# Unpadded head projections spread by DMA, refilled rounds, and a line attention that starts during the loads

## The chip, the cores and the metric

The kernel runs on one core of a Trainium2 chip. The metric is the device time of one execution in microseconds (us).

## The reference

Two layers of a decoder on x, 16 batches of 112 tokens by 256 features, with a context of 16 x 375 x 128. Each layer is: an attention, a cross attention to the context, and a mixture of eight experts, each added to x after a layer norm.

```
x = x + line_attention(norm(x))                # layer 0: 16 heads, causal, Pluecker lines
x = x + cross(norm(x), ctx)                    # 16 heads of 16: softmax(q k^T / 4) v, then Wo
x = x + experts(norm(x))                       # top 2 of 8
x = x + linear_attention(norm(x))              # layer 1
x = x + cross(norm(x), ctx)
x = x + experts(norm(x))                       # top 1 of 8
# cross: q = x Wq + bq, k = ctx Wk + bk, v = ctx Wv + bv (layer 1 without the biases)
```

## The kernel before

Everything is float32. Stages follow one another, each a block with a program per engine and a barrier behind it: load_constants, line_attention (or linear_attention in layer 1), cross_attention, route, experts, combine.

**load_constants** (L178) starts x as one DMA and then nineteen of weights on SyncE's queue, and the context as four DMAs on ScalarE's. TensorE turns each batch's context in three transposes (L232), ScalarE and VectorE copy them into cT in turn (L222, L263). VectorE takes the statistics of all 16 batches of x (L257, L260). After a wait for all twenty (L265), TensorE makes two constant rows crow (bias of the values through the output weights, plus the output bias), one for each attention of layer 0, and VectorE scales the query weights by a quarter. Then the stage ends.

**line_attention** (L274) begins with the row scales on GpSimd (L153, L155), one row normed on VectorE (L160), and runs NB + 5 steps in which batch t is turned and projected (L335, L377), batch t - 1 gets its line coordinates on VectorE and their inverse norms by a power on GpSimd (L558), batch t - 2 its scores and exponentials, t - 3 its values and t - 4 its output product. GpSimd also adds the constant row to x (L555).

**cross_attention** (L562) is built from rounds. Head h lives on partition strip 32 * (h % 4): its 16 features lie on the first 16 partitions of the strip, and the weights are padded on the host with zero columns (head_columns, L1613), so that a projection of 128 columns gives four heads in place. A key projection of batch b is four products (keys, L680, `kT`), the queries eight (L668, `qT`). A round (round_of, L619) is the pair of score products of one batch (L610), whose maximum VectorE takes (L848), and the six transposed score products of the batch before it (L616), whose exponential ScalarE takes (L768). The maxima enter the transposed scores as a 17th row: the key side has ones there from its padded bias, the query side has the negated maxima, spread into a padded row tile (nmp, L862), turned by four transposes (L697, shift_turn) and added to the queries in `qs` (shifted_queries, L868). Scores have one pair of PSUM banks and so have the transposed scores: each round waits for the maximum and the exponential of the round before.

Eight rounds make the step of one batch. In step t, slots 0 to 4 take the score pairs 3 to 7 of batch t + 1 and slots 5 to 7 the pairs 0 to 2 of batch t + 2. Between the rounds TensorE has the rest, called filler here: values (L652), the turns of x (L661), keys, queries, context values (L690), the turn of the maxima, and of the output its turns and product (L705, L711, L717). The order is written out by hand:

```python
for t in range(-2, NB + 1):
    round_of(t, 0)   # behind it: values(t-1,3), x_turn(t+2)
    round_of(t, 1)   # keys(t+2,0), queries(t+2)
    round_of(t, 2)   # values(t,0), u_turn(t-1), keys(t+2,1)
    round_of(t, 3)   # keys(t+2,2)
    round_of(t, 4)   # values(t,1), out_turn(t-1), keys(t+2,3)
    round_of(t, 5)   # context_values(t+1,0) and (t+1,1)
    round_of(t, 6)   # values(t,2), out_product(t-1), context_values(t+1,2), shift_turn(t+1)
    round_of(t, 7)   # nothing
```

ScalarE copies keys (L784), context values (L791), turned x (L773), u and the output (L797, L802) between the exponentials, in layer 1 also the queries (L778); VectorE copies the queries in layer 0 (L856), normalises and adds the output to x. GpSimd adds the constant row. SyncE has nothing to do in this stage.

Of the kernel before, what the change touches and what calls it, by code (L numbers as in the profile page):

```python
# [177 lines left out]
def load_constants(nc, g, A):  # L178

    ph = Phase(nc, "load")  # L180
    s_x, s_w, s_pool, s_dve = ph.sem("x", "w", "pool", "dve")
    s_ctx = ph.sem("ctx0", "ctx1", "ctx2", "ctx3")
    turned, act_copied, dve_copied = ph.sem("turned", "act_copied", "dve_copied")
    made = ph.sem("made")
    bv = ph.sb("bv", [P, 4])
    bvb = ph.sb("bvb", [P, 4, S])
    spread = ph.sem("spread")
    st = ph.sb("st", [S, NB, 6])
    cin = ph.sb("cin", [CT, NB, NC3, CD])
    bt = [ph.ps(f"t{u}", [P, 512]) for u in range(4)]  # L190
    with nc.Block() as block:
        @block.sync
        def _(sp):
            sp.dma_start(g.x[:, :, :], A["x"].rearrange("b t d -> t b d")).then_inc(s_x, 16)
            sp.dma_start(g.w_l0[:, :, :], A["w_l0"].rearrange("(c p) n -> p c n", p=P)).then_inc(s_w, 16)
            sp.dma_start(g.wo_l0[:, :, :], A["wo_l0"].rearrange("(c p) n -> p c n", p=P)).then_inc(s_w, 16)
            for l in range(2):
                sp.dma_start(g.wq_x[:, l], A["wq_x"][l].rearrange("(c p) n -> p c n", p=P)).then_inc(s_w, 16)
                sp.dma_start(g.wo_x[:, l], A["wo_x"][l].rearrange("(c p) n -> p c n", p=P)).then_inc(s_w, 16)
                sp.dma_start(g.wr[:, l], A["wr"][l].rearrange("(c p) n -> p c n", p=P)).then_inc(s_w, 16)  # L200
            sp.dma_start(g.wk_x[:, :, :], A["wk_x"].rearrange("l p n -> p l n")).then_inc(s_w, 16)
            sp.dma_start(g.wv_x[:, :, :], A["wv_x"].rearrange("l p n -> p l n")).then_inc(s_w, 16)
            sp.dma_start(g.bq_x[:, :], A["bq_x"]).then_inc(s_w, 16)
            sp.dma_start(g.bk_x[:, :, :], A["bk_x"]).then_inc(s_w, 16)
            sp.dma_start(g.rows[:, :, :], A["rows"].rearrange("(o r) d -> o r d", o=1)).then_inc(s_w, 16)
            sp.dma_start(g.w_l1[:, :, :, :], A["w_l1"].rearrange("(c p) r n -> p c r n", p=P)).then_inc(s_w, 16)
            sp.dma_start(g.wo_l1[:, :, :], A["wo_l1"].rearrange("(c p) n -> p c n", p=P)).then_inc(s_w, 16)
            sp.dma_start(g.lepe[:, :, :], A["lepe"].rearrange("(m p) n -> p m n", p=P)).then_inc(s_w, 16)
            sp.dma_start(g.rope[:, :, :], A["rope"].rearrange("r t d -> t r d")).then_inc(s_w, 16)
            sp.dma_start(g.br[:, :, :], A["br"].rearrange("(o l) e -> o l e", o=1)).then_inc(s_w, 16)  # L210
            sp.dma_start(g.b2[:, :, :], A["b2"].rearrange("l e d -> e l d")).then_inc(s_w, 16)
            sp.dma_start(bv[:, :], A["bv"]).then_inc(s_w, 16)
            sp.wait_ge(s_w, 16 * 20)

        @block.scalar
        def _(act):
            for n in range(4):
                act.dma_start(cin[:, 4 * n:4 * n + 4].rearrange("p b c d -> p (b c) d"),
                              A["ctx"][4 * n:4 * n + 4].rearrange("b (c p) d -> p (b c) d", p=CT)).then_inc(s_ctx[n], 16)
            for b in range(0, NB, 2):  # L220
                act.wait_ge(turned, b + 1)
                act.activation(g.cT[:, b, :], bt[b % 4][:, 0:CL], ACT.Copy).then_inc(act_copied, 1)  # L222

        @block.tensor
        def _(pe):
            pe.wait_ge(s_pool, 3)
            for b in range(NB):
                if b % 4 == 0:
                    pe.wait_ge(s_ctx[b // 4], 16)
                reused(pe, (act_copied, dve_copied)[b % 2], (b - 4) // 2 + 1)  # L230
                for c in range(NC3):
                    last = pe.transpose(bt[b % 4][:, c * CT:(c + 1) * CT], cin[:, b, c, :], g.ident[0:CT, 0:CT])  # L232
                last.then_inc(turned, 1)
            pe.wait_ge(s_w, 16 * 20)
            pe.wait_ge(act_copied, NB // 2)
            pe.wait_ge(spread, 1)
            for r in range(2):
                for c in range(2):
                    pe.matmul(bt[0][0:S, r * D:(r + 1) * D], bvb[:, 2 * r + c, :],
                              g.wo_l0[:, c, :] if r == 0 else g.wo_x[:, 0, c, :], start=(c == 0), stop=False)  # L240
                pe.matmul(bt[0][0:S, r * D:(r + 1) * D], g.ones[0:1, 0:S], g.rows[0:1, r, :],
                          start=False, stop=True).then_inc(made, 1)

        @block.gpsimd
        def _(pool):
            pool.memset(g.ident[:, :], 0.0).then_inc(s_pool, 1)
            pool.memset(g.ones[:, :], 1.0).then_inc(s_pool, 1)
            pool.memset(g.nhalf[:, :], -0.5)
            pool.wait_ge(s_pool, 1)
            pool.affine_select(g.ident[:, :], g.ident[:, :], [[-1, P]], ALU.not_equal, 1.0, base=0,  # L250
                               channel_multiplier=1).then_inc(s_pool, 1)

        @block.vector
        def _(dve):
            dve.wait_ge(s_x, 16)
            for b in range(NB):
                dve.bn_stats(st[:, b, :], g.x[:, b, :]).then_inc(s_dve, 1)  # L257
            for b in range(NB):
                dve.wait_ge(s_dve, b + 1)
                dve.bn_aggr(g.mv[:, b, :], st[:, b, :])  # L260
            for b in range(1, NB, 2):
                dve.wait_ge(turned, b + 1)
                dve.tensor_copy(g.cT[:, b, :], bt[b % 4][:, 0:CL]).then_inc(dve_copied, 1)  # L263
            dve.wait_ge(s_w, 16 * 20)
            dve.tensor_copy(bvb[:, :, :], bv[:, :].unsqueeze(2).to_broadcast([P, 4, S])).then_inc(spread, 1)  # L265
            dve.wait_ge(made, 2)
            dve.tensor_copy(g.crow[:, :, :].rearrange("t r d -> t (r d)"), bt[0][0:S, 0:2 * D])
# [1396 lines left out]
```

## Time and profile before

| | us |
|---|---|
| median of 3 runs | 1896.82 |
| lowest, highest | 1896.57, 1900.24 |
| profiled execution | 1897.62 |
| its span | 1895.9 |

| engine | busy us | share of the span |
|---|---|---|
| TensorE, matmul | 1479.1 | 78% |
| TensorE, weight load | 1150.2 | 61% |
| VectorE | 802.7 | 42% |
| ScalarE | 584.7 | 31% |
| GpSimd | 348.0 | 18% |

Busy time is summed over stages with different limits. Matmuls are pipelined, so a busy TensorE isn't TensorE at its peak. A float32 product shows as two instructions. The granted clock is given as a share: 1.00 is 2.4 GHz and 0.50 is 1.2 GHz. In waits and timelines the part behind "<-" names what ended the idle time before an instruction.

### The profile page before, as it was taken

How to read it: one execution, taken by the hardware profiler on the slowest of the kernel's cores; microseconds unless marked ns; L12 is line 12 of the kernel's file. 1: busy time of each engine (PE TensorE's matmuls, PEld its weight loads, DVE VectorE, ACT ScalarE, POOL GpSimd, SP SyncE). 2: the span in 40 equal slices, each digit the busy share in tenths (PEclk: the TensorE clock that was granted, in tenths of full speed). 3: DMA queues.
4: the chain of work that ended last, by engine and by line, in shares of the span. 5: the costliest groups of instructions: out<-in, count | busy, mean ns of one | idle time of the engine just before them, and what ended most of it. 6: DMA issues, size and time to landing. Idle time of an engine off the chain costs nothing. (4 is left out here: it accounts for less than half of the span.)

```text
span 1895.9 us, 36053 instructions
## 1 busy us (share of the span) xinstructions
PE 1479.1 (78%) x14148; PEld 1150.2 (61%) x14148; DVE 802.7 (42%) x1935; ACT 584.7 (31%) x1278; POOL 348.0 (18%) x432
## 2 busy tenths in 40 slices
PE   0578779999997649999945666658999998649993
PEld 0355536667665539999923545536676676549991
DVE  1355534555552142222255666644545542132226
ACT  0166614554543112222201211114555554112220
POOL 0366510000000112323253111100000000112314
PEclk9699979999997569999957887759999998559995
DMA  7000000000000138898720000000000000138862
GB/s 184 20 1 2 2 1 2 2 2 2 2 2 1 39 152 330 319 333 320 291 65 17 0 0 0 1 1 1 2 2 2 2 2 2 39 146 323 327 250 80
DMA packets 39069, 154.82 MB, mean 82 GB/s; under 512 B 5311, under 2 KB 27167, under 8 KB 31776
## 3 DMA queue, kind: packets, MB, share of 16 engines
q0 software_dynamic: 13056, 130.53, 18.8%
q1 hardware_dynamic: 19868, 19.42, 3.5%
q10 hardware_dynamic: 6020, 3.07, 0.6%
q8 instruction: 95, 1.56, 0.3%
q14 instruction: 30, 0.25, 0.0%
HBM read 140.16 MB, written 12.85 MB: 81 GB/s over the span
## 5 line engine op out<-in xcount | busy, mean ns | idle before, releaser
L848 DVE TENSOR_REDUCE xa_mx<-xa_ps_s 112x2 f32<-112x750 f32 x256 | 240.3, 939 | 260.1 <-PE xa_ps_s L610 259.6
L616 PE MATMUL xa_ps_p<-xa_qs,xa_kT 32*125 32x112 f32 x3072 | 241.8, 289 | 59.7 <-DVE xa_mx L848 48.7
L616 PEld LDWEIGHTS xa_ps_p<-xa_qs,xa_kT 32*125 32x125 f32 x3072 | 198.6, 190 | 140.7 <-issue 69.5
L768 ACT ACTIVATE xa_p<-xa_ps_p 125x672 f32<-125x672 f32 x256 | 186.9, 730 | 226.5 <-PE xa_ps_p L616 226.5
L610 PE MATMUL xa_ps_s<-xa_kT,xa_qT 32*112 32x375 f32 x1024 | 232.2, 530 | 9.4 <-DVE xa_mx L848 9.2
L1439 PE MATMUL ex_ps_h<-ex_xT,ex_w 128*128 128x128 f32 x1792 | 212.8, 278 | 13.1 <-DMA ex_w<-in_experts,ex_now 13.0
L1439 PEld LDWEIGHTS ex_ps_h<-ex_xT,ex_w 128*128 128x128 f32 x1792 | 212.0, 195 | 17.0 <-DMA ex_w<-in_experts,ex_now 13.8
L1449 PE MATMUL ex_ps_y<-ex_w,ex_hT 128*128 128x256 f32 x896 | 202.7, 379 | 0.0
L1449 PEld LDWEIGHTS ex_ps_y<-ex_w,ex_hT 128*128 128x128 f32 x896 | 166.0, 190 | 20.1
L1472 ACT ACTIVATE ex_hT<-ex_ps_h,ex_w 128x128 f32<-128x128 f32 x224 | 69.9, 363 | 290.4 <-PE ex_ps_h L1439 290.4
L1484 DVE TENSOR_SCALAR ex_hT<-ex_ps_h,ex_w 128x128 f32<-128x128 f32 x224 | 68.2, 346 | 175.1 <-PE ex_ps_h L1439 150.3
L680 PE MATMUL xa_ps_a<-cT,wk_x 128*128 128x375 f32 x256 | 113.4, 527 | 0.1
L652 PE MATMUL xa_ps_o<-xa_p,xa_v 125*17 125x112 f32 x3072 | 102.4, 268 | 1.7 <-ACT xa_p L768 1.7
L153 POOL TENSOR_SCALAR rstd<-mv 112x16 f32<-112x16 f32 x6 | 1.7, 286 | 548.1 <-POOLq L77 452.4
L558 POOL TENSOR_TENSOR line_inv<-line_ss,nhalf 112x32 f32<-112x32 f32 x16 | 87.1, 5444 | 53.6 <-DVE line_ss L487 53.6
L1492 DVE COPY ex_y<-ex_ps_y 128x256 f32<-128x256 f32 x56 | 23.7, 424 | 167.6 <-PE ex_ps_y L1449 167.6
L784 ACT ACTIVATE xa_kT<-xa_ps_a,bk_x 128x375 f32<-128x375 f32 x128 | 73.4, 573 | 62.5 <-PE xa_ps_a L680 61.9
L610 PEld LDWEIGHTS xa_ps_s<-xa_kT,xa_qT 32*112 32x112 f32 x1024 | 71.4, 172 | 20.4 <-issue 10.4
L1553 PE MATMUL cb_ps_b<-b,wtT 8*112 8x256 f32 x64 | 36.5, 675 | 53.8 <-DVE cb_sum L1561 43.8
L652 PEld LDWEIGHTS xa_ps_o<-xa_p,xa_v 125*17 125x17 f32 x3072 | 68.3, 99 | 16.6 <-ACT xa_p L768 2.1
L668 PEld LDWEIGHTS xa_ps_a<-xa_xT,wq_x 128*128 128x128 f32 x512 | 69.9, 212 | 10.0 <-issue 2.9
L1398 POOL COPY ex_now<-xrow 128x1 int32 (+1 forms) x58 | 10.6, 183 | 347.9 <-PE ex_ps_y L1449 228.8
(258 smaller groups left out, 2164.3 us busy)
## 6 DMA issues: line engine op xcount, KB each, us to landing
ys<-ex_y SPq DMA_DIRECT2D x56, 128.0 KB
xn<-rt_xn SPq DMA_DIRECT2D x8, 448.0 KB, 4.4
load_cin<-in_ctx ACTq DMA_DIRECT2D x4, 750.0 KB
x<-in_x SPq DMA_DIRECT2D x1, 1792.0 KB
out_x<-x SPq DMA_DIRECT2D x16, 112.0 KB
wq_x<-in_wq_x SPq DMA_DIRECT2D x2, 512.0 KB
w_l<-in_w_l SPq DMA_DIRECT2D x1, 1024.0 KB
ex_xg<-xn,ex_now POOLq DMA_INDIRECT x56
```

The lines of the kernel that those rows point to most:

```text
L558: pool.tensor_tensor(inv[:, b % 2], ss[:, b % 2], g.nhalf[:, :], ALU.pow).then_inc(inv_done, 1)
L610: return pe.matmul(bsc[0:S, i, 0:CL], qT[r:r + 32, b % 2, n, :], kT[r:r + 32, b % KB, n, :], start=True, stop=True)
L616: return pe.matmul(bp[0:CT, i, c * S:(c + 1) * S], kT[r:r + 32, b % KB, n, c * CT:(c + 1) * CT], qs[r:r + 32, b % 2, n, :], start=True, st ...
L652: last = pe.matmul(bo[32 * j:32 * j + HD + 1, n * S:(n + 1) * S], vb[:, b % VB, c, h, :], p[slot % 4][:, j % 2, c * S:(c + 1) * S], start= ...
L668: last = pe.matmul(ba[0][:, n * S:(n + 1) * S], g.wq_x[:, layer, c, n * P:(n + 1) * P], xT[:, c, :], start=(c == 0), stop=(c == 1))
L680: pe.matmul(ba[(1, 1, 0, 1)[n]][:, 0:CL], g.wk_x[:, layer, n * P:(n + 1) * P], g.cT[:, b, :], start=True, stop=True).then_inc(k_made, 1)
L768: act.activation(p[slot % 4][:, :, :], bp[0:CT, :, 0:NC3 * S], ACT.Exp).then_inc(exped, 1)
L784: act.activation(kT[:, b % KB, n, :], ba[(1, 1, 0, 1)[n]][:, 0:CL], ACT.Identity, bias=g.bk_x[:, layer, n:n + 1]).then_inc(k_copied, 1)
L848: dve.tensor_reduce(mx[:, b % 2, 2 * pair:2 * pair + 2], bsc[0:S, :, 0:CL], AX, ALU.max).then_inc(maxed, 1)
L1439: last = pe.matmul(bh[k][:, (j % 2) * SLOTS:(j % 2 + 1) * SLOTS], w[:, u, c * FF + j * P:c * FF + (j + 1) * P], xT[:, c, :], start=(c == 0 ...
L1449: last = pe.matmul(by[u % 2][:, 0:D], hT[:, u % 2, j, :], w[:, u, 2 * FF + FJ + j * D:2 * FF + FJ + (j + 1) * D], start=(j == 0), stop=(j ...
L1472: last = act.activation(hT[:, u % 2, 2 * k + i, :], bh[k][:, i * SLOTS:(i + 1) * SLOTS], ACT.Relu, bias=bias(u, 2 * k + i))
```

## The change

Load stage. It is gone as a stage. All loads are issued by SyncE inside the block of the line attention, in the order x (four DMAs of four batches, each with its own semaphore), the line weights, `bv` and `rows` (line_in), then the cross weights and the context (cross_in), then the rest. The context is turned on the host and loaded into cT directly. VectorE takes the statistics of four batches before the steps and of four more in each of steps 0, 1 and 2; GpSimd makes the row scales in four groups. The first constant row is made in step 0 of the line attention, behind the first projection, the second at the start of the first cross attention. The query weights are no longer scaled; the factor is in the copy of the queries.

Cross attention. Weights are unpadded. Keys are two products of 128 columns (eight heads each) copied to `kU`, queries four products copied by VectorE to `qU`. SyncE spreads them from there to the strips of `kT` and `qT` (three buffers each): eight DMAs per key half, eight for the queries, and four that put the negated maxima, turned by a single narrow transpose and copied by ScalarE to `nmT`, onto row 16 of each strip. The ones on the key side are from a memset of `kT`. `qs` and its addition are gone. Score products contract 16 rows and transposed ones 17. TensorE waits for the DMAs at rounds 0, 1 and 5. The filler is arranged anew and the loop begins one step earlier.

```diff
+def load_constants(sp, g, A):
+    for n in range(4):
+        rows = slice(4 * n, 4 * n + 4)
+        sp.dma_start(g.x[:, rows, :], A["x"][rows].rearrange("b t d -> t b d")).then_inc(g.x_in[n], 16)
+    sp.dma_start(g.w_l0[:, :, :], A["w_l0"].rearrange("(c p) n -> p c n", p=P)).then_inc(g.line_in, 16)
+    sp.dma_start(g.wo_l0[:, :, :], A["wo_l0"].rearrange("(c p) n -> p c n", p=P)).then_inc(g.line_in, 16)
...
+    for n in range(4):
+        sp.dma_start(g.cT[:, 4 * n:4 * n + 4, :], A["ctxT"][:, 4 * n:4 * n + 4, :]).then_inc(g.cross_in, 16)
...
# line attention, VectorE
+            row_stats(0)
...
             for t in range(NB + 5):
+                if t < 3:
+                    row_stats(t + 1)
+                if t == 1:
+                    dve.wait_ge(crow_made, 1)
+                    dve.tensor_copy(g.crow[:, 0, :], b_out[0:S, 0:D]).then_inc(crow_set, 1)
...
# cross attention, SyncE
+            def spread_k(b, m):
+                sp.wait_ge(k_copied, 2 * b + m + 1)
+                reused(sp, shifted, PAIRS * (b - RB + 1))
+                sp.wait_ge(ones_set, b % RB + 1)
+                for k in range(2):
+                    for j in range(4):
+                        i = 4 * k + j
+                        sp.dma_start(kT[32 * j:32 * j + HD, b % RB, 2 * m + k, :], kU[HD * i:HD * i + HD, b % 2, m, :]) \
+                            .then_inc(k_spread[RB * m + b % RB], 16)
...
+            def spread_nm(b):
+                sp.wait_ge(nm_copied, b + 1)
+                reused(sp, shifted, PAIRS * (b - RB + 1))
+                for j in range(4):
+                    sp.dma_start(qT[32 * j + HD:32 * j + HD + 1, b % RB, :, :], nmT[QUADS * j:QUADS * j + QUADS, b % 2, :]) \
+                        .then_inc(nm_spread[b % RB], 16)
+            for t in range(-2, NB):
+                if on(t + 2):
+                    spread_k(t + 2, 0)
+                    spread_q(t + 2)
+                if on(t + 1):
+                    spread_nm(t + 1)
+                if on(t + 2):
+                    spread_k(t + 2, 1)
# cross attention, TensorE
-                return pe.matmul(bsc[0:S, i, 0:CL], qT[r:r + 32, b % 2, n, :], kT[r:r + 32, b % KB, n, :],
+                return pe.matmul(bsc[0:S, i, 0:CL], qT[r:r + HD, b % RB, n, :], kT[r:r + HD, b % RB, n, :],
...
-                    if slot == 0:
-                        pe.wait_ge(qs_made, t + 1)
+                    if slot == 0:
+                        pe.wait_ge(nm_spread[t % RB], 16 * NM_DMAS * (t // RB + 1))
...
+                        pe.wait_ge(q_spread[sb % RB], 16 * Q_DMAS * (sb // RB + 1))
+                    if sp % 4 == 0:
+                        pe.wait_ge(k_spread[RB * (sp // 4) + sb % RB], 16 * K_DMAS * (sb // RB + 1))
```

The new order of the filler:

```python
for t in range(-3, NB + 1):
    round_of(t, 0)   # behind it: values(t-1,3), keys(t+2,0)
    round_of(t, 1)   # queries(t+2)
    round_of(t, 2)   # values(t,0), u_turn(t-1)
    round_of(t, 3)   # context_values(t+1,0) and (t+1,1)
    round_of(t, 4)   # values(t,1), context_values(t+1,2)
    round_of(t, 5)   # keys(t+2,1), shift_turn(t+1)
    round_of(t, 6)   # values(t,2), out_turn(t-1)
    round_of(t, 7)   # x_turn(t+3), out_product(t-1)
```

## Rows read from the trace of the kernel before

**Rows 1.** Timeline, load stage and first projection: start, us, engine, line, operation, count.

```profile
0.82 45.34 ACTq L218 DMA_DIRECT2D load_cin<-in_ctx  x4
...
0.82 0.39 SPq L194 DMA_DIRECT2D x<-in_x  x1
...
17.57 5.32 DVE L257 BATCH_NORM_STATS2 load_st<-x 112x6 f32<-112x256 f32 x16 [17.57 <-DMA x<-in_x]
...
60.22 0.38 DVE L265 COPY load_bvb<-load_bv 128x448 f32<-128x448 f32 x1
...
76.13 3.67 PE L377 MATMUL line_ps_b<-w_l,line_xT 128*112 128x512 f32 x4 [0.45 <-ACT line_xT L417]
```

**Rows 2.** Windows, load stage: busy of PE, PEld, DVE, ACT, POOL; clock, DMA, GB/s.

```profile
10.00:17.60 7.60, 0.00 (x0) 0.00 (x0) 0.03 (x1) 0.00 (x0) 0.00 (x0) 1.00 1.11 261
```

**Rows 3.** Timeline, ScalarE, copies of u: one per batch, first and second cross stage.

```profile
428.40 0.54 ACT L797 ACTIVATE xa_uT<-xa_ps_o 128x448 f32<-128x448 f32 x1
...
448.65 0.54 ACT L797 ACTIVATE xa_uT<-xa_ps_o 128x448 f32<-128x448 f32 x1
...
1495.59 0.54 ACT L797 ACTIVATE xa_uT<-xa_ps_o 128x448 f32<-128x448 f32 x1
...
1515.83 0.54 ACT L797 ACTIVATE xa_uT<-xa_ps_o 128x448 f32<-128x448 f32 x1
```

**Rows 4.** Timeline of one cross batch: a round with nothing behind it, and the next.

```profile
446.97 0.36 PE L616 MATMUL xa_ps_p<-xa_qs,xa_kT 32*125 32x112 f32 x2 [1.12 <-DVE xa_mx L848]
...
447.92 0.94 DVE L848 TENSOR_REDUCE xa_mx<-xa_ps_s 112x2 f32<-112x750 f32 x1 [1.09 <-PE xa_ps_s L610]
...
449.01 0.36 PE L616 MATMUL xa_ps_p<-xa_qs,xa_kT 32*125 32x112 f32 x2
```

**Rows 5.** Timeline, same batch: TensorE, queries, one filled round, the output product.

```profile
430.33 1.93 PE L668 MATMUL xa_ps_a<-xa_xT,wq_x 128*128 128x112 f32 x16
...
432.20 0.36 PE L616 MATMUL xa_ps_p<-xa_qs,xa_kT 32*125 32x112 f32 x2
...
433.04 0.77 PE L652 MATMUL xa_ps_o<-xa_p,xa_v 125*17 125x112 f32 x24
...
434.22 0.80 PE L680 MATMUL xa_ps_a<-cT,wk_x 128*128 128x375 f32 x2
...
434.95 0.36 PE L616 MATMUL xa_ps_p<-xa_qs,xa_kT 32*125 32x112 f32 x2
...
443.07 1.12 PE L717 MATMUL xa_ps_m<-wo_x,xa_aoT 128*112 128x256 f32 x4
```

**Rows 6.** Timeline and one line's view: what a DMA issue costs on SyncE.

```profile
21.77 0.53 SPq L204 DMA_DIRECT2D bk_x<-in_bk_x  x1
...
27.08 0.99 SPq L210 DMA_DIRECT2D br<-in_br  x1
...
L1513 SPq DMA_DIRECT2D ys<-ex_y x56: 332/332/377, 707.1 to 1848.3; - x56
```

**Rows 7.** Waits of SyncE: us in total, times, longest; the last store of the program.

```profile
SPq L1531 <- DMA out_x<-x: 1.4, 1, 1.4
```

**Rows 8.** Windows of the first cross stage: steady state, lead-in, tail (columns as in 2).

```profile
430.00:450.00 20.00, 18.43 (x271) 13.91 (x270) 10.65 (x18) 9.99 (x18) 0.72 (x1) 1.00 0.01 2
...
275.00:279.00 4.00, 3.49 (x14) 1.21 (x13) 2.44 (x5) 1.15 (x2) 0.72 (x1) 1.00 0.00 0
...
588.00:592.00 4.00, 3.18 (x43) 2.37 (x42) 0.00 (x0) 1.46 (x2) 0.00 (x0) 0.52 0.02 4
```

**Rows 9.** Timeline, start of the first cross stage and its first shifted scores.

```profile
246.80 0.26 POOL L153 TENSOR_SCALAR rstd<-mv 112x16 f32<-112x16 f32 x1 [19.98 <-SPq L604]
...
283.76 0.36 PE L616 MATMUL xa_ps_p<-xa_qs,xa_kT 32*125 32x112 f32 x2 [1.12 <-DVE xa_mx L848]
```

**Rows 10.** Timeline, tail of that stage: twelve shifted scores at the lower clock.

```profile
595.40 1.60 PE L616 MATMUL xa_ps_p<-xa_qs,xa_kT 32*125 32x112 f32 x12 [0.83 <-ACT xa_p L768]
```

**Rows 11.** Timeline: the power that makes the row scales, sixteen columns.

```profile
70.16 2.95 POOL L155 TENSOR_TENSOR rstd<-rstd,nhalf 112x16 f32<-112x16 f32 x1
```

More of the change, by code:

```diff
@@ L147, in persistent @@
     g.yrow = sb("yrow", [S, 2, NB], I32)
+    g.loads = Phase(nc, "loads")
+    g.x_in = g.loads.sem("x0", "x1", "x2", "x3")
+    g.line_in, g.cross_in, g.rest_in = g.loads.sem("line", "cross", "rest")
     return g
@@ L175, in add_to_x @@
     dve.tensor_copy(g.mv[:, bass.ds(b, 1), :], mv).then_inc(s_x, 1)
[L178 to L267, printed above, removed]
-            dve.tensor_scalar(g.wq_x[:, :, :, :].rearrange("p l c n -> p (l c n)"),
-                              g.wq_x[:, :, :, :].rearrange("p l c n -> p (l c n)"), CROSS_SCALE, None, ALU.mult)
-            dve.tensor_scalar(g.bq_x[:, :], g.bq_x[:, :], CROSS_SCALE, None, ALU.mult)
-    ph.close()
@@ L318, in line_attention, with _ @@
     with nc.Block() as block:
+        @block.sync
+        def _(sp):
+            load_constants(sp, g, A)
         @block.tensor
@@ L385, in u_turn, with constant_row @@
                 last.then_inc(u_turned, 1)
-            pe.wait_ge(set_v, 5)
-            pe.wait_ge(set_p, 2)
+            def constant_row():
+                pe.wait_ge(spread, 1)
+                for c in range(2):
+                    pe.matmul(b_out[0:S, 0:D], g.bvb[:, c, :], g.wo_l0[:, c, :], start=(c == 0), stop=False)
+                pe.matmul(b_out[0:S, 0:D], g.ones[0:1, 0:S], g.rows[0:1, 0, :], start=False, stop=True).then_inc(crow_made, 1)
+            pe.wait_ge(ident_set, 3)
             for t in range(NB + 5):
@@ L718, in out_product @@
                 last.then_inc(out_made, 1)
-            pe.wait_ge(set_v, 2)
-            pe.wait_ge(set_p, 1)
-            for t in range(-2, NB + 1):
+            pe.wait_ge(set_v, 2 - layer)
+            pe.wait_ge(v_set, 1)
+            if layer == 0:
+                pe.wait_ge(g.cross_in, 16 * CROSS_DMAS)
+                for c in range(2):
+                    pe.matmul(bm[0:S, 0:D], g.bvb[:, 2 + c, :], g.wo_x[:, 0, c, :], start=(c == 0), stop=False)
+                pe.matmul(bm[0:S, 0:D], g.ones[0:1, 0:S], g.rows[0:1, 1, :], start=False, stop=True).then_inc(crow_made, 1)
+            for t in range(-3, NB + 1):
                 round_of(t, 0)
@@ L804, in _ @@
             act.activation(warm[:, :], g.mv[:, 0, 0:1], ACT.Exp)
-            for t in range(-2, NB + 1):
+            for t in range(-3, NB + 1):
                 if on(t):
```

353 lines of the change are left out of this document (209 added, 144 removed).

## The prediction

> **What bounds the kernel now.** The profiled execution took 1897.62 us with a span of 1895.9, so 1.7 us lie around the span; the median of the runs shown is 1896.82, 0.8 us under it. The sum is made against 1897.6 and then carried to the median unchanged. I read the time by stage, because the change touches only some: the load stage, both cross attentions, and the entry of the line attention. Router, experts, combine and linear attention keep their code.
>
> The load stage is a wait. x is read as one transfer and lands at 17.6 us, the last of the twenty weights lets VectorE go on at 60.2, the context occupies ScalarE's queue for 45 us, and the first projection of the line attention starts at 76.1 [rows 1]. TensorE has nothing to win here; what counts is which bytes the first projection really needs.
>
> The cross attentions take one batch each 20.25 us in both layers [rows 3] at the full clock, with TensorE busy 18.4 of 20 us against 10.7 and 10.0 for VectorE and ScalarE [rows 8]. A batch is eight rounds. A round with nothing behind it takes 2.04 us: 446.97 to 449.01, the loop from the scores over VectorE's 0.94 us maximum back to the same PSUM banks [rows 4]. A round with filler takes 0.84 us (432.20 to 433.04) plus the filler: the next starts at 434.95, 2.75 us on, after values, four turns and one key product [rows 5]. So up to 1.2 us of filler per round is free and the rest is paid. Before, filler is bunched: eight bare rounds are 16.3 us, and the 3.9 us to 20.25 are filler above the free amount in four rounds, while one is empty.
>
> **The change, part by part.**
>
> *Less filler, spread.* Four padded key products become two, at 0.73 us each (434.22 to 434.95), sixteen query passes become eight, 1.87 us (430.33 to 432.20) to some 0.93, and four turns of the maxima become one narrow one [rows 5]. By slot the filler is then: slot 0 values and keys, 0.77 + 0.73 = 1.50; slot 1 queries, 0.93; slot 2 values and four turns, 1.18 (433.04 to 434.22); slot 7 the output product and two turns, about 1.2 by its 1.12 [rows 5]; slots 3 to 6 a pair of small products each, under 1.2 by the same prices. Only slot 0 exceeds the free amount: 0.84 + 1.50 = 2.34, and seven at 2.04 give 16.6 us. What hides the filler is VectorE's loop; it must keep its own extra work (queries 0.4 us, normalise, finish) inside the gaps of a round, which 10.7 busy us in 16.6 allow.
>
> *28 DMAs per batch on SyncE.* Eight for each key half, eight for the queries, four for the row of maxima. Their operands must land before a round, where before a VectorE or ScalarE copy in place sufficed. Price of an issue: 0.33 us where the queue is free, 0.53 and 0.99 for two small ones of the load stage, the latter onto a single partition [rows 6]. I take 0.36 with the step between two (0.04) for the 24 wide ones, which look like the first, and 0.57 for the four that write one partition; the bounds are 0.36 and 1.0. From the end of an issue to its landing: the last store is waited for 1.4 us [rows 7]; a small copy inside SBUF can hardly need more, and I let it go to 2. The queue order is keys 0, queries, maxima, keys 1, and SyncE waits in that order, so a late maxima row delays keys 1 behind it. Two paths: (a) round 0 to keys 0 copied, about 3.1 us (an estimate: the burst, values and product of rows 5, then ScalarE's copy); 16 issues 5.8; landing 1.4: 10.3, due for round 5, which starts at 2.34 + 4 x 2.04 = 10.5. Just hidden. (b) From round 5 to the maxima copied 2.65 us (an estimate: burst and key product of rows 5, then ScalarE's exponential and two short copies), four issues 2.3, eight issues 2.9, landing 1.4: 9.2 us; it is due for round 1 of the next step, 3 x 2.04 + 2.34 = 8.5 after round 5. So 0.7 us shows, and a batch takes 17.3. With all issues at 0.36 it is 8.4, hidden: 16.6. With 1.0 for the four it is 10.9: 19.0.
>
> Thirteen batches per layer run in this state: 13 x (20.25 - 17.3) = 38 us, 77 for both layers.
>
> *The prologue.* From the start of the stage to the first shifted scores are 37.0 us now [rows 9]. The new one has the DMAs in series with nothing to cover them: 16 issues and a landing, 7.2 us, before the first score, and the maxima row, 3.7 us, before the first shifted score; the shorter projections and the overlap of the second batch's give part back. Bounds 2 and 8, I take 6 per layer, 12. In the first layer the constant row (three products and a copy) moved here from the load stage: 3 us. The gain of the cross stages is 77 - 12 - 3 = 62.
>
> The Trainium skill, "DMA: Bandwidth & Descriptors", section "Rules for kernel authors", speaks against this part: small transfers are to be coalesced, since under 64 KB one pays mostly overhead, and "Anatomy of one DMA" puts a fixed 2 us on each. The last store's 1.4 us [rows 7] is below it. By the page's 2 us path (b) ends 0.6 us later and the batch is an estimated 17.9 us.
>
> *Load stage.* The first projection needs x and the line weights. In order on one queue are now x, 512 KB and 256 KB and two small ones, 2.56 MB in all, ahead of everything else; at the 261 GB/s of the stretch before x landed [rows 2] 9.8 us, plus 0.8 at the start and 1.4 landing: 12. At two thirds of that rate it is 17. I take 14 for the first projection instead of 76.1 [rows 1]: 62 us. Row statistics and scales of the first four batches lie before it: four statistics at a sixteenth of 5.3 us each, and a power of four columns under the 2.95 of sixteen [rows 11], all done about 10 us. Given back: the other twelve statistics on VectorE, 3 x 2 us, three powers of about 1.2 on GpSimd, which already carries that loop, and the constant row of 3 us on TensorE before the second turn. I take 8 (bounds 3 and 14). The later weights and the context (now 128 partitions, no transposes, no copies) have 170 us to land. Gain 62 - 8 = 54, bounds 45 and 62. The memsets of the key tiles are on GpSimd beside the row scales' wait; cover gone, they would cost some 1.5 us once.
>
> **Sum:** 1897.6 - 62 - 54 = 1781.6; I give 1781.
>
> **The rivals.**
>
> *The SyncE queue sets the batch.* Issues at 0.47 instead of 0.36 and at 1.0 for the four, landing 2: path (b) is 2.65 + 4 + 3.8 + 2 = 12.5, the batch 8.16 + 12.5 = 20.6, so the cross stages lose 9 + 15, and only the load gain is left: 1868. Half of that surcharge, a batch of 19, gives 1897.6 - (32 - 15) - 54 = 1826. For it: four rows of the load stage over 0.9 would fit; against: fifty-six stores at 0.332 with 128 rows each [rows 6].
>
> *TensorE falls to the lower clock in the steady state* (the slower side). What holds the clock is not shown by busy time alone: it stood at 1.00 in the lead-in with 3.49 of 4 us busy and fell to 0.52 in the tail with 3.18 of 4, where only shifted scores and values ran [rows 8]. Now contractions are 16 and 17 rows high instead of 32 and full-array projections are halved. At the lower clock twelve shifted scores take 1.60 us [rows 10] while the whole burst with its scores lasts 0.84 now [rows 5], so a burst is some 1.6 and the 9 us of filler per batch about 16: 12.8 + 16 = 29 us, 26 x 8.7 = 226 us more, 1897.6 + 226 + 15 - 54 = 2085. It is slower than before from a mean batch of 21.8 us on, that is when four batches in ten run at the lower clock ((21.8 - 17.3) / (29 - 17.3)). Against: rounds are fuller, 15.5 busy of 17.3.
>
> The Trainium skill, "TensorE: Matmul & The Clock Gate", section "HAM oscillation — how this bites in real kernels", has the same effect for idle gaps between bursts; the lead-in and tail [rows 8] agree that the level moves with what TensorE did before.
>
> *The early start does not deliver.* If the 17.6 us of x [rows 1] is the queue's pace and not shared with the context, the projection starts at 26: 12 us less, 1793; with 14 given back 1799.
>
> *Strips of 16 or 17 rows do not run side by side.* Then the change does not do what it says and the bursts double: about 1.7 us a round, 8 x 0.85 more where not hidden, batch 23 or so, 1897.6 + 72 + 15 - 54 = 1930. Against: values of 17 columns share the array, 24 in 0.77 us [rows 5].
>
> **How the numbers follow.** Forecast (batch 16.6 to 18, load 45 to 62): 1750 to 1810, 0.62. SyncE sets the batch: 0.20, 1815 to 1868. Early start short: 0.08. Lower clock: 0.06. Strips: 0.04. 1781 is the first. The range 1745 to 1832 takes the first, the third and half of the second and leaves out 0.2. Faster 0.89, within 0.2% (what a measurement of this kernel can tell from no change) 0.01, slower 0.10, the last two rivals.
>
> **What would show it.** ScalarE's copies of u 16.6 to 17.5 us apart; keys' and maxima's DMA waits on TensorE under 1 us per batch; SyncE's issues near 0.33; the first projection near 14 us and the line attention's later batches as far apart as before; the clock 1.00 in the steady state. Wrong would be copies 19 us or more apart, with TensorE waiting for DMA at rounds 0, 1 and 5, or a clock near 0.5 in the middle of a cross stage.

## The result, and the profile after

The changed kernel takes 2138.9 us (median of four, 2135.8 to 2142.6) against 1897.1 us (the median of the kernel before, with one run more than in its table): 1.128 times as long, 95% interval 1.126 to 1.129. The forecast was 1781. The profiled execution has a span of 2140.4 us, 244.5 more than the 1895.9 before.

The page of the changed kernel, its first lines and the products of the cross attention (busy us, mean ns of one, idle before):

```profile
span 2140.4 us, 35951 instructions
PE 1787.9 (84%) x13620; PEld 1335.5 (62%) x13620; DVE 782.3 (37%) x1909; ACT 547.4 (26%) x1222; POOL 357.6 (17%) x444
PEclk8995555555555559999858887555555555558995
L648 PE MATMUL xa_ps_s<-xa_kT,xa_qT 16*112 16x375 f32 x1024 | 403.0, 884 | 28.0 <-DMA xa_qT<-xa_qU 20.8
L654 PE MATMUL xa_ps_p<-xa_qT,xa_kT 17*125 17x112 f32 x3072 | 405.3, 429 | 22.0 <-DMA xa_qT<-xa_qU 7.9
```

TensorE does less work than before and is busy for longer: the clock row stands at 5 tenths over both cross stages. Before, the steady state was at 1.00 [rows 8]. Windows of the changed kernel in the first cross stage (us, busy of PE, PEld, DVE, ACT, POOL, then the granted clock):

```profile
300.00:360.00 60.00, 60.00 (x519) 42.53 (x522) 20.05 (x32) 18.85 (x34) 1.45 (x2) 0.50 0.08 19
360.00:420.00 60.00, 60.00 (x524) 42.67 (x518) 20.05 (x32) 18.85 (x34) 1.45 (x2) 0.50 0.08 19
454.00:458.00 4.00, 3.94 (x69) 3.22 (x68) 2.80 (x6) 1.33 (x2) 0.00 (x0) 1.00 0.15 36
458.00:462.00 4.00, 3.19 (x46) 2.06 (x46) 1.99 (x3) 2.46 (x5) 0.00 (x0) 1.00 0.12 27
462.00:466.00 4.00, 0.81 (x12) 0.84 (x14) 0.00 (x0) 0.00 (x0) 0.00 (x0) 0.68 0.09 18
466.00:470.00 4.00, 4.00 (x31) 2.50 (x25) 0.94 (x1) 1.44 (x3) 0.00 (x0) 0.50 0.00 0
```

60.00 of 60 us busy at 0.50 is the lower of the clock's two levels (1.2 GHz), with no gap to blame. Twice it rose for some 10 us, once in each cross stage. The first time is at 454 to 462: there the rounds follow each other as planned, and then a transfer comes late. The timeline of that stretch:

```profile
454.88 0.57 PE L648 MATMUL xa_ps_s<-xa_kT,xa_qT 16*112 16x375 f32 x2
457.00 0.57 PE L648 MATMUL xa_ps_s<-xa_kT,xa_qT 16*112 16x375 f32 x2
459.03 0.57 PE L648 MATMUL xa_ps_s<-xa_kT,xa_qT 16*112 16x375 f32 x2
458.25 5.64 SPq L624 DMA_DIRECT2D xa_qT<-xa_qU  x8
465.19 0.55 PE L654 MATMUL xa_ps_p<-xa_qT,xa_kT 17*125 17x112 f32 x2 [3.94 <-DMA xa_qT<-xa_qU]
```

A batch is read from ScalarE's copies of u (a batch's products with its values, before they are divided by the sums), as in [rows 3]; the first three and the last of the first layer:

```profile
272.67 0.54 ACT L834 ACTIVATE xa_uT<-xa_ps_o 128x448 f32<-128x448 f32 x1 [0.45 <-PE xa_ps_o L689]
303.15 0.54 ACT L834 ACTIVATE xa_uT<-xa_ps_o 128x448 f32<-128x448 f32 x1 [0.45 <-PE xa_ps_o L689]
332.74 0.54 ACT L834 ACTIVATE xa_uT<-xa_ps_o 128x448 f32<-128x448 f32 x1 [0.45 <-PE xa_ps_o L689]
703.99 0.54 ACT L834 ACTIVATE xa_uT<-xa_ps_o 128x448 f32<-128x448 f32 x1 [2.52 <-PE xa_ps_o L689]
```

The first step is 30.5 us, and from then on nearly every step of both layers is 29.6, where 20.25 stood before. The load part, by contrast, did what was asked. The timeline of the changed kernel: first projection, start of the cross stage, the constant row, the first scores and the first shifted scores.

```profile
12.63 3.72 PE L324 MATMUL line_ps_b<-w_l,line_xT 128*112 128x512 f32 x4 [2.64 <-DMA rows<-in_rows]
188.52 0.20 ACT L841 ACTIVATE xa_warm<-mv 112x1 f32<-112x1 f32 x1 [4.22 <-PEq L76]
192.17 2.02 PE L757 MATMUL xa_ps_m<-wo_x,bvb 128*112 128x256 f32 x4 [5.76 <-POOL xa_v L947]
210.28 1.59 PE L648 MATMUL xa_ps_s<-xa_kT,xa_qT 16*112 16x375 f32 x4 [10.44 <-DMA xa_qT<-xa_qU]
242.76 0.55 PE L654 MATMUL xa_ps_p<-xa_qT,xa_kT 17*125 17x112 f32 x2 [0.57 <-DVE xa_mx L879]
```

So the 244.5 us divide as follows (us; "u" is a batch's copy of u, and the last column is the last kernel of the experiments):

| interval | before | changed | last experiment |
|---|---|---|---|
| to the first cross stage | 246.8 | 188.5 | 188.4 |
| stage start to first u, layer 0 | 60.1 | 84.2 | 71.4 |
| first to last u, layer 0 | 302.9 | 431.3 | 264.4 |
| last u to first u of layer 1 | 703.6 | 725.5 | 712.6 |
| first to last u, layer 1 | 301.5 | 430.4 | 260.0 |
| last u to the end | 281.0 | 280.5 | 281.7 |
| span | 1895.9 | 2140.4 | 1778.4 |

58.3 us are gained in the load part, 46.0 lost on the way into the two stages (24.1 and 21.9), 257.3 lost from copy to copy. On the way in, the first scores wait 10.44 us for the query copies, as the row above shows, and the whole stretch runs at 0.50.

### The profile page after: what moved, and what is told of

Read it like the earlier page. It is cut to its first block and busy times, and to the rows that moved or that the text cites. A ratio compares the mean times of both kernels' runs of the same rounds, so it can differ in the third digit from the quotient of the medians.

```text
span 2140.4 us, 35951 instructions
## 1 busy us (share of the span) xinstructions
PE 1787.9 (84%) x13620; PEld 1335.5 (62%) x13620; DVE 782.3 (37%) x1909; ACT 547.4 (26%) x1222; POOL 357.6 (17%) x444
## 5 line engine op out<-in xcount | busy, mean ns | idle before, releaser
L654 PEld LDWEIGHTS xa_ps_p<-xa_qT,xa_kT 17*125 17x125 f32 x3072 | 338.4, 315 | 162.3 <-issue 123.9
L648 PE MATMUL xa_ps_s<-xa_kT,xa_qT 16*112 16x375 f32 x1024 | 403.0, 884 | 28.0 <-DMA xa_qT<-xa_qU 20.8
L654 PE MATMUL xa_ps_p<-xa_qT,xa_kT 17*125 17x112 f32 x3072 | 405.3, 429 | 22.0 <-DMA xa_qT<-xa_qU 7.9
L1486 PEld LDWEIGHTS ex_ps_y<-ex_w,ex_hT 128*128 128x128 f32 x896 | 165.9, 190 | 20.2
L689 PE MATMUL xa_ps_o<-xa_p,xa_v 125*17 125x112 f32 x3072 | 167.0, 384 | 0.0
L648 PEld LDWEIGHTS xa_ps_s<-xa_kT,xa_qT 16*112 16x112 f32 x1024 | 114.3, 278 | 45.0 <-DMA xa_qT<-xa_qU 22.8
L689 PEld LDWEIGHTS xa_ps_o<-xa_p,xa_v 125*17 125x17 f32 x3072 | 106.5, 137 | 33.4 <-issue 25.9
L706 PE MATMUL xa_ps_k<-cT,wk_x 128*128 128x375 f32 x128 | 103.3, 911 | 0.0
L954 POOL TENSOR_TENSOR x<-x,crow 112x256 f32<-112x256 f32 x16 | 11.6, 724 | 412.7 <-DVE xa_xn L164 412.7
L725 PE MATMUL xa_ps_x<-wv_x,cT 128*125 128x256 f32 x128 | 75.7, 693 | 0.0
L1004 PE MATMUL lin_ps_b<-ident,lin_xn 112*128 112x112 f32 x32 | 9.2, 388 | 72.0 <-DVE lin_xn L164 72.0
## 6 DMA issues: line engine op xcount, KB each, us to landing
xa_kT<-xa_kU SPq DMA_DIRECT2D x512, 23.4 KB, 1.9
```

The costliest lines, as they stand in the source:

```text
L648: return pe.matmul(bsc[0:S, i, 0:CL], qT[r:r + HD, b % RB, n, :], kT[r:r + HD, b % RB, n, :], start=True, stop=True)
L654: return pe.matmul(bp[0:CT, i, c * S:(c + 1) * S], kT[r:r + HD + 1, b % RB, n, c * CT:(c + 1) * CT], qT[r:r + HD + 1, b % RB, n, :], start ...
L689: last = pe.matmul(bo[32 * j:32 * j + HD + 1, n * S:(n + 1) * S], vb[:, b % VB, c, 4 * n + j, :], p[slot % 4][:, j % 2, c * S:(c + 1) * S] ...
L706: pe.matmul(bk[:, 0:CL], g.wk_x[:, layer, m * P:(m + 1) * P], g.cT[:, b, :], start=True, stop=True).then_inc(k_made, 1)
L725: pe.matmul(bank[0:CT, 0:D], g.cT[:, b, c * CT:(c + 1) * CT], g.wv_x[:, layer, :], start=True, stop=True).then_inc(v_made, 1)
L1486: last = pe.matmul(by[u % 2][:, 0:D], hT[:, u % 2, j, :], w[:, u, 2 * FF + FJ + j * D:2 * FF + FJ + (j + 1) * D], start=(j == 0), stop=(j ...
```

## The experiments

Theory H (the height of the contraction): products over 16 and 17 rows, with half of the full-array products gone, do not keep the clock up, however busy TensorE is. Rival F: the halved filler alone does it. Rival Q: the waits for SyncE's copies and the long empty start let the clock fall. A cost beside them, whatever the clock, is the SyncE queue itself. A batch below is the usual distance of two copies of u, and the clock is read in stretches of 20 us. "Filler" says how much full-height key and query work a batch has against the kernel before: "doubled" is the changed kernel's half, issued twice. e1, e2 and e6 to e9 have one run each, e3, e4, e5 and e10 four; the kernel before, run beside them, had medians of 1897.9 to 1900.1 us, and ratios below are to these, with their 95% intervals.

| kernel | rows | filler | copies | clock in the steady state | batch, us | time, us |
|---|---|---|---|---|---|---|
| before | 32 | full | none | 1.00 | 20.25 | 1897 |
| e1 | 16/17 | full | none | 1.00, later 0.74 to 0.93 | 20.2, later 23 | 1994 |
| changed | 16/17 | half | 28, SyncE | 0.50, two short rises | 29.6 | 2139 |
| e2 | 32 | half | 28, SyncE | 0.81 to 0.99 | 23.7 | 1969 |
| e9 | 16/17 | doubled | 28, SyncE | 0.50 to 1.00 | 24 to 36 | 2149 |
| e3 | 32 | half | 28, two queues | 1.00, at times 0.83 | 19.1 | 1834 |
| e4 | 32 | full | none | 1.00 | 20.2 | 1843 |
| e5 | 32 | half | 20, two queues | 1.00 | 18.1 | 1800 |
| e6 | 16/17 | half | as e5 | 0.50, two short rises | 29.6 | 2106 |
| e7 | 16/32 | half | as e5 | 1.00, at times 0.5 | 18, at times 28.7 | 1850 |
| e8 | 16/17 | doubled | as e5 | 1.00, once 0.91 | 18.9, at times to 21.5 | 1889 |
| e10 | 32 | half | 20, three queues | 1.00 | 17.3 | 1780 |

**e1: the height alone, in the kernel before.**

```diff
-  pe.matmul(bsc[0:S, i, 0:CL], qT[r:r + 32, ...], kT[r:r + 32, ...],
+  pe.matmul(bsc[0:S, i, 0:CL], qT[r:r + HD, ...], kT[r:r + HD, ...],
...
-  pe.matmul(bp[0:CT, i, ...], kT[r:r + 32, ...], qs[r:r + 32, ...], ...)
+  pe.matmul(bp[0:CT, i, ...], kT[r:r + HD + 1, ...], qs[r:r + HD + 1, ...], ...)
```

> The kernel before, in which only the height of the contraction in the two small products is changed: scores 16 rows instead of 32, shifted scores 17 instead of 32. The rows left out hold zeros, so instruction counts, columns and results stay. Theory H (the height): products of 16 and 17 rows, side by side, do not hold the clock. It expects the granted clock near 0.5 in both cross stages, the copies of u some 33 to 35 us apart (18.4 busy us of the batch nearly double) instead of 20.25, and 2250 to 2300 us. Rival F (filler: the halved full-array projections) and rival Q (waits for the new DMAs let the clock fall) expect the clock at 1.00 and 1897 us, since this kernel has neither.

1993.8 us, 96 more for leaving out rows that hold zeros. Windows of its first cross stage:

```profile
345.00:365.00 20.00, 18.43 (x272) 13.80 (x270) 10.66 (x17) 10.20 (x18) 0.72 (x1) 1.00 0.01 2
385.00:405.00 20.00, 18.52 (x227) 13.73 (x229) 9.28 (x15) 9.23 (x17) 0.72 (x1) 0.83 0.00 1
525.00:545.00 20.00, 19.31 (x209) 14.56 (x212) 7.55 (x12) 8.18 (x15) 0.72 (x1) 0.74 0.00 1
```

Up to 385 us it is the same kernel as before, busy time and all, at 1.00; then the clock goes up and down, and most batches take 22 to 25 us. Rivals F and Q, which both said 1897, are out as the whole cause; so is H in its strong form, which said 0.5 throughout and 2250 to 2300. The height has an effect, and full filler resists it.

**e2: the changed kernel with 32 rows.** The queries' slot is zeroed by GpSimd once a batch.

```diff
+  pool.memset(qT[:, b % RB], 0.0).then_inc(q_zeroed, 1)
...
-  qT[r:r + HD, b % RB, n, :], kT[r:r + HD, b % RB, n, :],
+  qT[r:r + 32, b % RB, n, :], kT[r:r + 32, b % RB, n, :],
```

> The changed kernel with both small products contracted over 32 rows again: the slot of the queries is zeroed by one GpSimd memset a batch, the key pads hold ones, so the rows added contribute zero. DMAs, filler and order stay. Theory H expects the clock at 1.00 for most of both cross stages and a batch set by SyncE's chain at its measured issue cost of 0.63 us, 20 to 22 us: 26 x (29.6 - 21) = 224 us less than 2139, near 1915. Rival F expects the clock to stay at 0.50 and 2139. Rival Q expects 0.50 as long as TensorE waits 4 us for a DMA in some batches, so also near 2139, or a mixture.

1968.7 us: 170 of the 241.8 us of the loss come back with two heights changed in the products, though GpSimd does more. Rival F, which said 2139, is out here too. Its windows, and the waits of TensorE in 300 to 420 (us in total, times, longest):

```profile
300.00:360.00 60.00, 47.85 (x688) 35.19 (x684) 25.95 (x41) 24.10 (x45) 2.32 (x4) 0.91 0.09 21
360.00:420.00 60.00, 45.48 (x634) 33.84 (x626) 25.16 (x40) 22.57 (x41) 3.48 (x6) 0.89 0.11 25
```

```profile
PE xa_ps_p L655 <- issue: 18.3, 5, 4.2
PE xa_ps_p L655 <- DMA xa_qT<-xa_qU: 6.6, 5, 1.5
```

Busy share is lower than in the changed kernel (46.7 of 60 against 60.00) and the clock higher. The rows put 18.3 us to "issue", idle time for which the profile shows no releaser. These waits stand before the rounds that need the second key half, fall to 6.0 us in the same stretch of e3, where SyncE issues sixteen copies a batch, and are gone in e5, where it issues twelve; that they are waits for the second key half is inferred from this. A batch is 23.7 us, not the 20 to 22 expected; how much of the excess is the queue and how much the clock of 0.9 was not separated.

**e3: two queues.** e2 with the twelve copies of queries and maxima issued by GpSimd.

```diff
-  sp.dma_start(qT[32 * j:32 * j + HD, b % RB, k:QUADS:2, :], qU[HD * i:HD * i + HD, b % 2, :, :])
+  pool.dma_start(qT[32 * j:32 * j + HD, b % RB, k:QUADS:2, :], qU[HD * i:HD * i + HD, b % 2, :, :])
...
-  sp.dma_start(qT[32 * j + HD:32 * j + HD + 1, b % RB, :, :], nmT[QUADS * j:QUADS * j + QUADS, b % 2, :])
+  pool.dma_start(qT[32 * j + HD:32 * j + HD + 1, b % RB, :, :], nmT[QUADS * j:QUADS * j + QUADS, b % 2, :])
```

> As the run before it (32-row contractions), and the eight query copies and four maxima copies of each batch are issued from GpSimd's queue, so that SyncE issues only the 16 key copies, at 0.63 us each 10.1 us a batch. Theory H with the SyncE chain as the second cost: clock 1.00 and a batch of 16.6 to 18 us, so 1897 - 26 x 2.8 + 15 - 58 = 1780, range 1760 to 1820. If issues on GpSimd cost as much as on SyncE and the maxima's path stays late, 19 us a batch and 1830. Rival F expects 0.50 and about 2100.

1834.3 us (ratio 0.966, interval 0.964 to 0.968), 19.1 us a batch: above the 1760 to 1820 of the theory and at the 1830 given for late maxima. A window of it:

```profile
300.00:360.00 60.00, 50.36 (x767) 36.27 (x765) 31.07 (x52) 28.48 (x53) 21.84 (x42) 1.00 0.12 28
```

GpSimd's issues are cheaper than SyncE's (504 ns for the queries, 524 for the maxima, against 589), and a batch still waits for the queries (1.0 to 1.4 us), for the second key half by the inference above (1.2 to 1.4) and in part of the batches for the maxima (up to 1.7).

**e4: the new load part with the old cross attention.** In the changed kernel the whole cross attention is the old one again, the scaling aside, which is now done as the queries are copied.

```diff
-  kU = ph.sb("kU", [P, 2, 2, CL])
-  qU = ph.sb("qU", [P, 2, 2, S])
...
+  qs = ph.sb("qs", [P, 2, QUADS, S])
```

> The load stage and the line attention of the changed kernel with the cross attention of the kernel before (padded projections, 32-row contractions, no copies between partitions; the scaling of the query weights is moved into the copy of the queries, and the constant rows are made where the changed kernel makes them). It measures the load part alone: the first cross stage began 58.3 us earlier in the changed kernel, so 1897 - 58 = 1839, 1835 to 1845 with the constant row in the first cross stage. If the load gain is given back in a later stage, it shows as a time nearer 1897. A clock of 1.00 and 20.25 us a batch in both cross stages is expected by every theory.

1843.1 us (0.971, 0.970 to 0.973), inside the range expected. Two of its copies of u:

```profile
353.26 0.54 ACT L799 ACTIVATE xa_uT<-xa_ps_o 128x448 f32<-128x448 f32 x1
373.51 0.54 ACT L799 ACTIVATE xa_uT<-xa_ps_o 128x448 f32<-128x448 f32 x1
```

The stage starts at 187.8, batches are 20.2 us apart at 1.00, and the two parts of the change are now separate: the load part is worth 55 us, the cross part costs 296 (2138.9 less 1843.1).

**e5: fewer copies.** One copy carries both key halves, so that eight do the work of sixteen; for that the second half's product moves one step earlier, and the maxima are back on SyncE. 32 rows.

```diff
-  sp.dma_start(kT[32 * j:32 * j + HD, b % RB, 2 * m + k, :], kU[HD * i:HD * i + HD, b % 2, m, :])
+  sp.dma_start(kT[32 * j:32 * j + HD, b % RB, k:QUADS:2, :], kU[HD * i:HD * i + HD, b % 2, :, :])
```

> The 32-row kernel with fewer and better spread copies: both key halves of a batch are projected before their copies, so that one copy carries both (8 instead of 16 a batch, on SyncE), the four maxima copies are on SyncE and the eight query copies stay on GpSimd. In the run before it the three waits of a batch were 1.4 us (queries), 0.2 to 1.7 us (maxima) and 1.3 us (second key half). Theory (32 rows hold the clock; what is left above the bare rounds is late copies): clock 1.00 in the steady state, 16.6 to 17.5 us a batch instead of 19.1, so 1834 - 26 x 2.1 = 1780, range 1765 to 1800. If a copy with twice the rows costs twice the issue (1.2 us), nothing is gained: 19 to 20 us and 1835 to 1850.

1800.5 us (0.947, 0.943 to 0.950), 18.1 us a batch, 0.6 above the range. A copy that carries both halves costs the same issue (595 ns against 589), so eight issues a batch are saved; what the merger alone is worth, without the other two moves, was not run. The Trainium skill, "DMA: Bandwidth & Descriptors", section "Rules for kernel authors", asks for small transfers to be coalesced; this trace agrees, by issues saved. One wait is left, the queries'; TensorE's waits in 280 to 400:

```profile
PE xa_ps_p L643 <- DMA xa_qT<-xa_qU: 8.7, 7, 1.6
```

**e6: e5 with 16 and 17 rows.**

```diff
-  qT[r:r + 32, b % RB, n, :], kT[r:r + 32, b % RB, n, :],
+  qT[r:r + HD, b % RB, n, :], kT[r:r + HD, b % RB, n, :],
...
-  kT[r:r + 32, b % RB, n, c * CT:(c + 1) * CT], qT[r:r + 32, b % RB, n, :],
+  kT[r:r + HD + 1, b % RB, n, c * CT:(c + 1) * CT], qT[r:r + HD + 1, b % RB, n, :],
```

> The kernel of the run before it in this set with one difference: the contractions are 16 rows (scores) and 17 rows (shifted scores) instead of 32; the rows left out hold zeros on the query side. Copies, queues, waits and filler are the same. Theory H (height, with the halved full-array filler): the clock stays at 0.50 through both cross stages, 29 to 30 us a batch, 2120 to 2140 us. Rival Q (waits for copies and the long empty prologue let the clock fall in the changed kernel): with most of those waits gone the clock is at 1.00 and the time that of the 32-row kernel within 5 us.

2105.8 us against 1800.5 for one difference. Its windows:

```profile
300.00:360.00 60.00, 58.60 (x547) 42.09 (x550) 20.73 (x33) 19.91 (x37) 10.98 (x22) 0.54 0.10 20
360.00:420.00 60.00, 60.00 (x523) 42.39 (x516) 20.52 (x34) 19.03 (x35) 10.33 (x20) 0.50 0.09 18
```

The clock had risen for one batch (22.6 us long) and fell again, around one wait of 1.3 us, where e5 keeps 1.00 through seven waits of up to 1.6 us; then 29.6 us a batch to the end of the layer. In layer 1 it rose once more, and there a batch took 17.6 us, near the forecast's 17.3:

```profile
1640.00:1660.00 20.00, 18.88 (x272) 13.76 (x267) 10.31 (x17) 9.38 (x18) 4.62 (x10) 0.92 0.13 27
```

So this kernel can run at either level; what made the clock rise there is open. As the main cause rival Q is refuted: taking most of the waits away recovers 33 of the 242 us and leaves the clock at 0.50 nearly throughout.

**e7: the scores alone at 16 rows**, on e5.

```diff
-  qT[r:r + 32, b % RB, n, :], kT[r:r + 32, b % RB, n, :],
+  qT[r:r + HD, b % RB, n, :], kT[r:r + HD, b % RB, n, :],
```

> As the 32-row kernel with merged copies, but the scores alone contract 16 rows; the shifted scores keep 32. It tells whether a part of the height is enough. A score has 375 columns and a pair of them is 750 column passes a round, four shifted-score strips side by side 672: if the clock follows the mean height of all passes, this lies halfway: clock alternating, 20 to 24 us a batch, 1870 to 1970 us. If either product alone holds the clock, 16.6 to 17.5 us a batch and the 32-row time; if both are needed, 0.50 and 2120 to 2140.

1850.4 us, where 1870 to 1970 was expected. Its windows, a good and a bad stretch:

```profile
360.00:420.00 60.00, 55.20 (x827) 40.21 (x826) 31.98 (x52) 29.79 (x56) 15.52 (x30) 0.96 0.14 27
420.00:480.00 60.00, 59.17 (x688) 42.40 (x687) 27.83 (x45) 24.90 (x45) 15.51 (x30) 0.73 0.14 27
```

Between the two cases, but much nearer the 32-row kernel (1800.5) than e6 (2105.8), and mostly at 1.00. So the clock does not simply follow the mean height of all products, as the expectation had it. The shifted scores alone at 17 rows were not run.

**e8: e6 with the filler of the kernel before.** Every key and query product is issued twice into the same place.

```diff
+  for again in range(2):
+      last = pe.matmul(bk[:, 0:CL], g.wk_x[:, layer, m * P:(m + 1) * P], g.cT[:, b, :], ...)
...
-  for m in range(2):
+  for m in (0, 1, 0, 1):
```

> As the kernel with 16 and 17 rows and merged copies, but every key product and every group of query products is issued twice with the same operands into the same place, so that the full-height filler per batch is again that of the kernel before (four key products, sixteen query passes); results do not change. Theory H with the filler as its second part: the clock rises for part of the time as in the kernel before with 16 and 17 rows (0.83 to 1.00 by stretches, 22 to 25 us a batch), so 1930 to 2030 us although more work is done. If only the height of the small products matters, 0.50 and more work: 31 to 33 us a batch and 2180 to 2220 us.

1888.5 us: 192 more products than e6 (384 instructions), none of them needed, and 217 us less. Windows and two copies of u:

```profile
300.00:360.00 60.00, 58.80 (x846) 43.10 (x850) 31.06 (x50) 29.36 (x55) 15.46 (x30) 1.00 0.14 27
420.00:480.00 60.00, 58.23 (x833) 42.72 (x829) 31.73 (x51) 29.11 (x55) 16.61 (x32) 1.00 0.14 28
```

```profile
346.19 0.54 ACT L823 ACTIVATE xa_uT<-xa_ps_o 128x448 f32<-128x448 f32 x1
365.11 0.54 ACT L823 ACTIVATE xa_uT<-xa_ps_o 128x448 f32<-128x448 f32 x1
```

Steadier and faster than expected (22 to 25 us a batch). Height and filler thus act together: with these copies, low products with half the filler stay near 0.50, and either one restored brings the clock back. It also bears on e1, which has the same heights and as many full-height projections but alternates. There the filler is bunched and rounds stand bare; that this is the reason is likely, and was not tried by itself.

**e9: the changed kernel with doubled filler.**

```diff
+  for again in range(2):
+      last = pe.matmul(bk[:, 0:CL], g.wk_x[:, layer, m * P:(m + 1) * P], g.cT[:, b, :], ...)
...
+  for m in (0, 1, 0, 1):
```

> The changed kernel itself with one difference: every key product and every group of query products is issued twice with the same operands into the same place, so the full-height filler per batch is again four key products and sixteen query passes. Heights of 16 and 17 rows, all 28 copies on SyncE and their waits stay. If the missing filler alone keeps it at the lower clock, the clock rises and the batch is set by SyncE's chain: 22 to 24 us and 1940 to 1990, faster than 2139 although more work is done. If the waits for SyncE's copies are needed as well for the fall, it alternates as the changed kernel with 32 rows did (clock 0.81 to 0.93, 23.7 us a batch): 1970 to 2050. If the height alone keeps it down, 0.50 and 31 to 33 us a batch: 2180 to 2220.

2148.7 us, in none of the three ranges: the clock alternates, as the second said, but lower and with batches of 24 to 36 us, 100 us above its time; from the changed kernel's 2139 one run does not tell it apart. Windows:

```profile
360.00:420.00 60.00, 54.01 (x537) 38.34 (x536) 20.14 (x33) 18.60 (x34) 1.45 (x2) 0.70 0.08 19
540.00:600.00 60.00, 50.55 (x660) 36.69 (x660) 24.56 (x40) 23.19 (x44) 2.18 (x3) 0.92 0.09 22
```

Doubled filler holds 1.00 in e8 and not here, and what differs is the copies, their queues and the waits for them (up to 3.7 us for the queries between 300 and 600 us, 1.3 in e8). So rival Q has a share after all: it cannot explain the 0.50, but where the products are low the late copies undo what the filler brings. Which of the differences does it was not tried.

**e10: three queues.** e5 with two of the eight query copies issued by ScalarE and six by GpSimd, and a wait moved out of the stage's start; 32 rows.

```diff
-  for j in range(4):
+  for j in range(3):
       pool.dma_start(qT[32 * j:32 * j + HD, b % RB, k:QUADS:2, :], qU[HD * i:HD * i + HD, b % 2, :, :])
...
+  act.dma_start(qT[96:96 + HD, b % RB, k:QUADS:2, :], qU[HD * i:HD * i + HD, b % 2, :, :])
```

> The 32-row kernel with merged copies (1800.5 us, 18.1 us a batch), in which two of the eight query copies of a batch are issued by ScalarE and six by GpSimd, and the wait for the ones column of the values stands only before the first round with shifted scores instead of before the first products of the stage. The wait left was for the query copies, 1.2 us a batch; two issues fewer on GpSimd end its queue 1.0 us sooner. Expected: 17.0 us a batch, 26 x 1.1 = 29 us less, and 2 to 6 us per stage start: 1765 (1755 to 1780). If ScalarE's two issues (1.2 us) delay its exponentials, the rounds lengthen instead and the time stays at 1795 to 1810.

1779.9 us (0.939, 0.937 to 0.941), the fastest of all and at the upper end of the range; a batch is 17.3 us, not the 17.0 expected. Window, waits of TensorE in 280 to 400, and two copies of u:

```profile
300.00:360.00 60.00, 57.38 (x893) 41.50 (x888) 34.40 (x55) 32.43 (x61) 13.28 (x26) 1.00 0.15 31
```

```profile
PE xa_ps_p L644 <- ACT xa_p L794: 2.8, 7, 0.7
PE xa_ps_p L644 <- DVE xa_mx L880: 1.4, 7, 0.2
```

```profile
311.69 0.54 ACT L833 ACTIVATE xa_uT<-xa_ps_o 128x448 f32<-128x448 f32 x1
328.98 0.54 ACT L833 ACTIVATE xa_uT<-xa_ps_o 128x448 f32<-128x448 f32 x1
```

No wait for a DMA is left in that stretch; the rounds run by VectorE's and ScalarE's loops, 17.3 us a batch.

## Why the prediction was wrong, point by point

- **The clock**, the step that failed. The forecast priced every cross batch at the full clock, and the changed kernel ran them at 0.50: 29.6 us a batch instead of 17.3. The mechanism was among the rivals and was put at 0.06; its 29 us a batch came out well, and its burst of 1.6 us at the lower clock is in the trace (from 465.19 to the key product at 466.73). The sentence that dismissed it was "Against: rounds are fuller, 15.5 busy of 17.3", which judged the clock by busy share right after [rows 8] had been read as showing that busy share alone does not decide it. The changed kernel is at 60.00 of 60 busy and 0.50, e2 at 46.7 of 60 and 0.9. The lead-in, cited there as evidence, had 32-row and full-array products and said nothing of 16 rows. It was not at 1.00 throughout either; the kernel before, around the window of [rows 8]:

```profile
260.00:280.00 20.00, 16.55 (x60) 7.93 (x62) 8.59 (x11) 3.23 (x7) 0.72 (x1) 0.74 0.00 1
```

  The Trainium skill, "TensorE: Matmul & The Clock Gate", Part 1, says that the gate follows how busy TensorE has been; read as the busy time of the profile, that would give the full clock here, and the trace disagrees.
- **The rival's sum**, 2085, is 57 short of the profiled execution (2142.1 us; the median lies 3 lower). 31 are the steps between copies of u, 226 taken and 257.3 measured; 31 the entries, 46.0 against 15, as they too run at the lower clock; less 4 for the larger load gain.
- **The filler budget** was right: at 1.00 the changed kernel's rounds start at 454.88, 457.00 and 459.03, 2.1 and 2.0 us apart against 2.04 taken [rows 4]. Strips of 16 and 17 rows do run side by side.
- **SyncE's issue price** was mis-sized: 0.36 us was taken from wide stores to DRAM [rows 6], and the copies between partitions took 0.59 each, some 0.63 with the step to the next. The same queue of the kernel before had small loads well above the two that were read, this one of 6 KB:

```profile
24.17 1.70 SPq L208 DMA_DIRECT2D lepe<-in_lepe  x1
```

  One line's view in the changed kernel, the query copies (issue min/median/max in ns):

```profile
L624 SPq DMA_DIRECT2D xa_qT<-xa_qU x256: 585/593/1507, 203.9 to 1794.9; - x128
DMA to landing us min/median/max: 1.8/1.8/3.5
```

  The landing (1.8 from the start of the issue, 1.2 from its end) was under the 1.4 taken and the one-partition price (596 ns) near the 0.57. The fixed 2 us that the prediction quotes from the Trainium skill stand there in the section on DMAs that GpSimd issues; these are SyncE's and land 1.8 us after the start. With 0.63 the prediction's path (b) is 2.65 + 2.5 + 5.0 + 1.2 = 11.4 us against 8.5, so the batch would be 19.5; e2, at a clock of some 0.9, shows 23.7. The rival "the SyncE queue sets the batch" deserved more than 0.20. The bounds, 0.36 and 1.0, did hold the price; the value taken did not.
- **The entries** were sized at 12 + 3 us. e4 gives 3.9 for the constant row and what else moved into the first stage. With the copies and 32 rows e10 has 11.2 in layer 0 and 9.0 in layer 1, 20.2 in all; at the lower clock it was 46.0.
- **The load part** was right: first projection at 12.63 (14 predicted, 76.1 before [rows 1]), the stage 58.3 us earlier (54 predicted), of 63.5 gained 5.2 given back (8 predicted). The wait that ended last before the projection was the one for the small rows at the end of the line's own transfers (2.64 us), not x.
- **The steady state by itself**: 17.3 us a batch was forecast and e10 has it, by other means (32 rows, twenty copies, three queues). Its terms against the forecast's: load 58.4 (54), cross stages 38.5 + 41.5 = 80 (77), entries 20.2 lost (15), the end 0.7 lost; 1778.4 of span. The forecast of 1781 priced a kernel whose clock holds and whose copies are hidden, not the one at hand. That e10 comes within 1 us of it is partly luck: it is another kernel, and errors of 3 to 5 us in three terms cancel.
